# A GNN, linear-attention and Haar-FFN layer on one core: the next step's transposes and their copy to SBUF stand in front of the second mlp product instead of behind it

## The reference

```python
xn = layernorm(x)
# gnn: agg[row] += h[col] over the 100,000 edges
h = relu(xn @ W1 + b1) @ W2 + b2;  gnn = h + segment_sum(h[dst], src)
# mix: linear attention (y), then an mlp on it
y = v + (attention(k, q, v) @ proj_w + proj_b)
mix = y + gelu(layernorm(y) @ mlp_w1 + mlp_b1) @ mlp_w2 + mlp_b2
x = x + gnn + mix
x = x + haar_ffn(layernorm(x))
```

## Time and profile before

| | |
|---|---|
| median of 3 runs | 1737.19 us (1735.87 to 1739.85) |
| span of the profiled execution | 1920.7 us |
| profiled execution's own time beside its span | not recorded apart from the span |
| PE busy | 1662.6 us, 87% |
| DVE, ACT, POOL busy | 1043.3, 818.4, 1036.4 us |
| mean granted TensorE clock | 0.947 of 2.4 GHz |

### The profile page before, as it was taken

How to read it: one execution, slowest core, us unless ns; L and a number is a source line. 1 busy time by engine, 2 the same in 40 slices (tenths; PEclk the granted TensorE clock), 3 DMA queues, 4 the chain that set the end, 5 groups by cost and what they waited for, 6 DMA issues and landing times.

```text
span 1920.7 us, 25102 instructions
## 1 busy us (share of the span) xinstructions
PE 1662.6 (87%) x8243; PEld 1266.1 (66%) x8243; DVE 1043.3 (54%) x2340; ACT 818.4 (43%) x1892; POOL 1036.4 (54%) x1131
## 2 busy tenths in 40 slices
PE   5999999888889888988898668878988888888997
PEld 4778878776567666766676546656666566656675
DVE  5999999972344444544444322322332322458797
ACT  1235445443233344444433334535544444435643
POOL 3033443346465666666666655666666666657310
PEclk8999999998899999999999879989999899989998
DMA  5123222223255555555555544555554555445432
GB/s 178 38 77 107 86 88 96 81 85 120 88 176 159 155 153 155 154 153 155 156 153 156 160 157 139 161 152 155 163 157 148 156 153 161 155 146 183 150 125 102
DMA packets 87427, 263.63 MB, mean 137 GB/s; under 512 B 18765, under 2 KB 20813, under 8 KB 87298
## 3 DMA queue, kind: packets, MB, share of 16 engines
q0 software_dynamic: 43456, 119.44, 22.4%
q1 hardware_dynamic: 43842, 142.59, 21.8%
HBM read 217.15 MB, written 44.80 MB: 136 GB/s over the span
## 4 chain that ended last, share of the span: by engine, by line
PE 50%; issue 15%; DVE 13%; another core or an unknown queue 9%; ACT 8%; POOL 3%; DMA 1%; DVEq 0%; POOLq 0%; ACTq 0%
PE bank L986 10%; DVE sb_weights L1465 5%; PE bank L995 5%; PE bank L934 4%; ACT sb_weights L1280 3%; PE bank L904 2%; PE bank L905 2%; PE turn_bank L880 2%; PE bank L906 2%; PE bank L880 2%; DVE sb_step L1646 2%; PE bank L730 1%; PE bank L728 1%; PE bank L729 1%
## 5 line engine op out<-in xcount | busy, mean ns | idle before, releaser
L612 POOL DMA_INDIRECT sb_weights<-hidden_rows,sb_weights x880 | 860.3, 978 | 480.5 <-issue 223.8
L1745 DVE TENSOR_TENSOR sb_acc<-sb_acc,bank 125x257 f32 x220 | 92.6, 421 | 388.3 <-PE bank L882 138.9
L1280 ACT ACTIVATE sb_weights<-sb_const,sb_weights 128x125 f16<-128x125 f16 x880 | 266.7, 389 | 84.0 <-remote 31.6
L986 PE MATMUL bank<-sb_weights,sb_step 128*128 128x250 f32 x800 | 205.6, 416 | 79.6 <-ACT sb_weights L1190 43.0
L986 PEld LDWEIGHTS bank<-sb_weights,sb_step 128*128 128x128 f32 x800 | 165.4, 212 | 112.3 <-ACT sb_weights L1190 46.5
L1745 DVE TENSOR_TENSOR sb_acc<-sb_acc,turn_bank 125x257 f32 x220 | 92.4, 420 | 263.1 <-remote 115.7
L995 PE MATMUL bank<-sb_weights,sb_step 128*125 128x512 f32 x400 | 179.8, 592 | 1.4 <-issue 1.4
L1465 DVE TENSOR_TENSOR sb_weights<-sb_weights 128x512 f32<-128x512 f32 (+3 forms) x256 | 164.2, 683 | 3.6
L1198 ACT ACTIVATE sb_step<-sb_step 125x256 f32<-125x256 f32 x100 | 50.2, 506 | 252.5 <-DVE sb_step L1638 245.0
L728 PE MATMUL bank<-sb_w_parts,sb_x_high 128*125 128x512 f32 (+1 forms) x400 | 139.9, 350 | 3.7 <-issue 3.4
L730 PE MATMUL bank<-sb_w_parts,sb_x_low 128*125 128x512 f32 (+1 forms) x400 | 135.8, 340 | 7.2 <-issue 7.1
(11 more groups left out here) (314 smaller groups left out, 3666.5 us busy)
## 6 DMA issues: line engine op xcount, KB each, us to landing
sb_step<-x SPq DMA_DIRECT2D x63, 500.0 KB
sb_step<-x_t SPq DMA_DIRECT2D x50, 500.0 KB
sb_weights<-hidden_rows,sb_weights POOLq DMA_INDIRECT x880
y_rows<-sb_step SPq DMA_DIRECT2D x25, 500.0 KB
sb_step<-y_rows SPq DMA_DIRECT2D x25, 500.0 KB
z_rows<-sb_step SPq DMA_DIRECT2D x25, 500.0 KB
sb_step<-z_rows SPq DMA_DIRECT2D x13, 500.0 KB
out<-sb_step SPq DMA_DIRECT2D x13, 500.0 KB
```

Source lines behind the costliest of these rows:

```text
L612: pool.indirect_dma_start(out=ring[:, n % RING * 2 + h, 0:HID], out_offset=None, in_=table, in_offset=bass.IndirectOffsetOnAxis(ap=row_of[ ...
L986: last = pe.matmul(bk[:, (c % 2) * 250:(c % 2) * 250 + 2 * P], mlp1_w[:, k, c * 128:(c + 1) * 128], hT3[:, t.s, k, :], start=k == 0, stop= ...
L1280: mm = act.activation(hit[q % 2][:, i, :], iota_h[:, :], ACT.Abs, bias=less_lane[:, q * BP + i // 2, i % 2:i % 2 + 1])
L1745: dve.tensor_tensor(dst, dst, (BE, BH)[n % 2][0:P, 0:RW], ALU.add).then_inc(g_add, 1)
```

## The change

Three edits. On PE, `transposes(a + 1)` moves from behind `mlp2(a, 1)` to behind `groups(counts[1])`, in front of `mlp2(a, 0)`. On ACT, `copy_hT(a + 1)` moves from the turn's end to right behind `gelus(a, 1)`, in front of the second lot of one-hot batches. And `features(a, i)` wait for one gelu less: for the gelu that last read their own bank. (The `x1_ok` wait that is dropped asks for a value of 1 in every turn in which it stood; that is where the semaphore begins.)

```diff
 def features(t, i):
     bk = (BA, BB)[i]
     pe.wait_ge(h_t, t.g * 2 + 3)
-    pe.wait_ge(feat_c, t.g * 2 + i + 1)
+    pe.wait_ge(feat_c, max(1, t.g * 2 + i))
...
                     groups(counts[1])
+                    if a + 1 < STEPS:
+                        transposes(steps[a + 1])
                     pe.wait_ge(z_ok, a + 1)
...
                     mlp2(steps[a], 1)
-                    if a + 1 < STEPS:
-                        pe.wait_ge(x1_ok, max(0, b + 2) + 1)
-                        transposes(steps[a + 1])
                     groups(counts[3])
...
                     gelus(steps[a], 1)
+                    if a + 1 < STEPS:
+                        copy_hT(steps[a + 1], hT3)
                     hits_until(ahead + sum(counts[0:2 if a == 2 else 3]))
...
-                if a + 1 < STEPS:
-                    copy_hT(steps[a + 1], hT3)
-                    if a == 1:
-                        roots(EARLY, NT, 13, 12, "other_roots")
+                if a == 1:
+                    roots(EARLY, NT, 13, 12, "other_roots")
```

## The result

| | median us | lowest to highest | runs |
|---|---|---|---|
| before | 1737.22 | 1732.93 to 1742.02 | 20 |
| after | 1732.64 | 1727.94 to 1739.28 | 20 |

The ratio is 0.9973, 95% interval 0.9963 to 0.9982. The change gains 4.6 us. I had forecast 1700 us and a range of 1668 to 1728; both are wrong.

What follows compares the result with a forecast made beforehand. PE's own work plus its gaps was taken to bound the kernel, mainly the mlp-stage wait before the features. (19.82 - 18.09 - 0.2) x 24 = 37 us off 1737.2 gave 1700 us, range 1668 to 1728.

Steps and rivals of the forecast that it cites:

- the base of the sum: Mlp stage: turns of 22.55 us with 3.23 PE idle, and an undisturbed turn of 19.82, from which savings were scaled.
- what an undisturbed turn looks like: Turn 16 of the mlp stage, 19.82 us, 18.09 without its two PE waits; three more of 22 within 0.3 us.
- (19.82 - 18.09 - 0.2) x 24 = 37: Mlp stage: saving per undisturbed turn, less 0.2 us, over 24 turns; 37 us, taken off 1737.2.
- the surplus: First profile's execution: 183.5 us longer than the median of the runs, most likely in PE gaps.
- The gathers take over: Rival, 17%: POOL's gathers in the mlp stage hold the turn at 18.9 us; gain 22 us, 1715 us.
- the ring lets POOL start 12 groups ahead: Argument against gathers limiting the mlp stage: a lead of 24 gathers or 31 us, PE gaining only 19 us on it.
- 0.58 + 1.15: PE idle in turn 16: 0.58 us before features 1 for a gelu, 1.15 before the next features for the copy.
- The 1.13 us a turn for the lower clock: Mlp stage: mean PE clock 0.95 taken as 24.8 us lost to the 1.2 GHz level, 1.13 a turn.
- The y load: Rival, 5%, slower: moved transposes wait for y rows, issued 8.8 us after mlp2 1's end and landing late; 1776 us.
- The slack of 3.4 us: Before the moved transposes: y normalised at 24.0 us, wanted at 27.4, so PE would not wait.
- the copy ahead of the one-hots: ACT: later one-hot batches cost nothing, mlp2 work covering them; without cover up to 2 us in 7 turns, 14 us.
- no idle before L986: Sign of being right: PE idle before the features under 15 us in the stage instead of 67.5, none by the copy.

Runs made afterwards that it cites:

- second profile of before: The kernel before profiled again, no edit: span 1739.6 us, profiled execution 1741.44 us, timed median on that chip 1738.11 us.
- half-gather pair: One gather a group in place of two, in the kernel before (1690.07 us, ratio 0.9744) and in the changed kernel (1673.61 us, 0.9639).
- gelu line alone: Kernel before with only the relaxed gelu wait of the features: 1734.81 us, ratio 0.9982.
- move alone: Changed kernel with the old gelu wait of the features, so only the transposes and their copy are moved: 1740.63 us, ratio 1.0019 to the kernel before.
- one-input additions: Changed kernel with VectorE's two additions a turn replaced by a copy and a multiplication by 1: 1921.3 us on the slow chip, 1729.13 us on a normal one.

## Why the prediction was wrong

**The step that failed is the base of the sum.** I read 22.55 us a turn with 3.23 idle, and took turn 16, 19.82 us, as "what an undisturbed turn looks like". In the second profile of before, 15 of these 22 turns take 18.5 to 18.8 us, and all 22 average 19.2. So the term (19.82 - 18.09 - 0.2) x 24 = 37 was mis-sized: with the gathers out of the way the change is worth 16.5 us, by the half-gather pair. With all gathers it is worth 4.6, since GpSimd and not PE paces the stage. The cause of the surplus was not the profiler, as I assumed. Span 1920.7 and the stops by "remote" fit the 1944-us chip, and I take the profile to be from such a chip; the trace does not name its chip, so this is argued, not shown. The warning stood in the table: a span 183.5 us above the median of runs that spread by 4. I scaled the gaps down when I should have asked which of them exist at all.

**The gathers take over** was the second step that failed, by its chance: PE's saved time was taken to reach the end of the kernel. I gave it 17% and a turn of 18.9 us. That floor was right: 1.274 us by 14.7 is 18.7, and 18.8 was measured. "Against: the ring lets POOL start 12 groups ahead" was wrong. A lead helps only an engine that pauses now and then; GpSimd has none to spend, since it issues almost without a break from 740 us to 1500 (179.7 us of idle before 589 gathers, 0.305 each). In every run with all gathers the kernel ends 124 to 125 us after its last gather started (1614.9 and 1739.6 before, 1607.1 and 1731.3 after, 1797.1 and 1921.8 on the other chip). That alone doesn't say who paces: with half of the gathers it is 125 to 126 us too. With the base corrected, this rival gives (19.2 - 18.9) x 24 = 7 us, near the 4.6.

**The copy.** "0.58 + 1.15" became 0.9 a turn, all of it the gelu wait. The copy's 1.15 us stand in the disturbed profile and not in the second one; the gelu line alone gave 3.3 us (1738.11 to 1734.81, interval 0.5 to 5.7), and the whole change 4.6 (3.1 to 6.4). The 1.13 us a turn for the lower clock were nothing either: the clock of the stage is 1.00 in both windows above.

**The y load.** The mechanism was right and its size off. I wrote that y is issued 8.8 us after mlp2 1's end. In the turn shown, mlp2 1 ends at 1298.1 and y is issued at 1312.41: 14.3 us, since the z store, issued while y's load is under way, lands 12.4 us later instead of 7. With 12.7 us to land and 1.5 to be normalised, y is there after 28.5 us, and the transposes want it at 27.4. The slack of 3.4 us was none, and PE waited 12.6 us before the transposes in one profile, 2.7 in the other. Removing that wait gained nothing, since the gathers stood behind it. I had written that gelu 0 is held with `norm_rows` "but PE isn't"; with the old gelu wait PE is, which makes the move alone slower.

**What held:** the copy ahead of the one-hots cost nothing (0.2 us before L879 by L1283); no idle before L986; clock 1.00 in the stage; turns within 18.3 to 19 on average. That the gain within an execution with such stops is larger held in sign: 31.5 us there, not 95. The Trainium skill (SBUF — State Buffer, "Who interferes with whom") says that a VectorE instruction with two SBUF inputs contends with a GpSimd instruction that reads SBUF. The trace agrees: beside the addition x + y a gather took 1.86 us instead of 0.95. I had used this only for the floor; how often the additions meet gathers turned out to carry a large part of the 4.6 us.

## What to carry to other kernels

- Before reading gaps in a profile, compare its span with the timed median. If they differ by more than the runs spread, get another profile; the gaps of the first are not the kernel's.
- Ask first which engine never pauses. An engine at 76% "busy" with the same 0.3 us between all its instructions is full, and it sets the end whatever the busiest engine waits for. Halving that engine's work shows what an edit elsewhere would be worth.
- Two edits of one change may need each other. Run each alone before crediting either.

## What the runs showed of the hardware

- The kernel before takes 1736.9 to 1738.1 us in all other comparisons and 1944 on one chip, with the same instruction durations (0.946 and 0.949 us a gather). The difference shows as stops of 1.7 us on GpSimd, 84 in one execution, ended by nothing in the records, and as longer waits behind them. Neither half the gathers' bytes (1921.75 us) nor one-input additions (1921.3) avoided them. Their cause is open.
- A gather of 128 rows takes GpSimd the same 0.95 us with rows of 1 KB or 512 B (0.946 and 0.945 us median, 1020 to 1480 us).
- VectorE's additions can fall into step with the gathers: in the second profile of before the same collision stands in seven turns in a row, 18.5 us apart. The changed order on the other engines leaves 4 to 6 long gathers beside that addition in place of 13.
